# Five of the twelve w_gate slices transposed by DMA in the condition stage instead of by TensorE

## The reference, cut to what matters

```python
out = jnp.einsum('bsd,bdh->bsh', x, W[cat_ids]) + b[cat_ids][:, None, :]   # condition layer
# FFN on xc = act_qdq(out); act_qdq rounds to 16 bits with ONE scale, the maximum over the whole tensor
# lpbq_dequant rounds a weight to 4 bits with a scale for each block of 32
up   = act_qdq(xc @ lpbq_dequant(w_up).T)
gate = act_qdq(xc @ lpbq_dequant(w_gate).T)
sig  = fixed_qdq_u16(sigmoid(gate))
gate = act_qdq(gate * sig)
o    = act_qdq(gate * up)
y    = x + o @ lpbq_dequant(w_down).T
```

## Time and profile before

| what | value |
|---|---|
| median of 3 runs | 962.78 us (962.12 to 963.32) |
| the profiled execution | 961.0 us, span 959.2 us |
| PE busy | 891.4 us (93%) |
| DVE busy | 655.0 us (68%) |
| ACT busy | 422.2 us (44%) |
| DMA | 254.32 MB, mean 265 GB/s |
| condition stage, with its end | 0 to 139 us of the span |
| gate stage | 142.5 to 394 us |

### The profile page before, as it was taken

The page is one execution under the profiler, slowest core; times in us unless marked ns, Lnnn a source line. Parts: engine busy times, 40 slices in busy tenths (PEclk is TensorE's granted clock), DMA queues, the critical chain, the costliest instruction groups (busy, mean ns, idle before and its releaser), DMA issues.

```text
span 959.2 us, 13055 instructions
## 1 busy us (share of the span) xinstructions
PE 891.4 (93%) x4723; PEld 477.6 (50%) x4723; DVE 655.0 (68%) x773; ACT 422.2 (44%) x454; POOL 3.1 (0%) x12
## 2 busy tenths in 40 slices
PE   8999999999999999999999999980079999999998
PEld 7999994444444444444444444430034444444443
DVE  2349869655667455289899889659986788775511
ACT  1112335223223232299898872229865544444000
POOL 0000000000000000000000000000000000000000
PEclk9999999999999999999999999995589999999999
DMA  8999962643574433789999635999977899987221
GB/s 346 383 406 322 326 238 99 174 154 121 173 253 132 135 129 121 220 315 423 412 385 383 247 139 218 408 421 402 418 286 256 298 339 350 343 303 284 87 88 66
DMA packets 81299, 254.32 MB, mean 265 GB/s; under 512 B 32050, under 2 KB 32050, under 8 KB 77170
## 3 DMA queue, kind: packets, MB, share of 16 engines
q1 hardware_dynamic: 46066, 198.72, 55.2%
q10 hardware_dynamic: 35200, 55.20, 16.5%
HBM read 173.94 MB, written 73.66 MB: 258 GB/s over the span
## 4 chain that ended last, share of the span: by engine, by line
PE 82%; DMA 6%; ACT 5%; DVE 4%; issue 2%; SPq 0%; ACTq 0%; POOL 0%; DVEq 0%
PE bank L807 16%; PE bank L809 16%; PE bank L808 16%; PE bank L751 12%; PE bank L842 5%; PE bank L843 5%; PE bank L844 5%; DMA up_extra<-up_scratch 3%; ACT umag L688 2%; DVE ocode L1308 2%; ACT ocode L707 2%; PE bank L737 1%; DMA gate_even<-gate_scratch 1%; DMA wt_down<-wparts 1%; PE bias_bank L843 1%
## 5 line engine op out<-in xcount | busy, mean ns | idle before, releaser
L594 ACT ACTIVATE stage<-bank 128x512 f32<-128x512 f32 x186 | 108.6, 594 | 213.1 <-PE bank L809 164.8
L1069 DVE TENSOR_REDUCE tile_max<-stage 128x1 f32<-128x1536 f32 (+1 forms) x62 | 108.4, 1748 | 34.4 <-ACT stage L594 31.2
L807 PE MATMUL bank<-xq_head,wt_up 128*128 x336 | 127.4, 379 | 0.9 <-ACT stage L594 0.9
L807 PE MATMUL bank<-xq_head,wt_gate 128*128 (+1 forms) x336 | 127.4, 379 | 0.3 <-DVE xq_head L1056 0.3
L808 PE MATMUL bank<-xq_head,wt_up 128*128 x336 | 127.3, 379 | 0.0
L809 PE MATMUL bank<-xq_head,wt_up 128*128 x336 | 127.3, 379 | 0.0
L808 PE MATMUL bank<-xq_head,wt_gate 128*128 (+1 forms) x336 | 127.3, 379 | 0.0
L809 PE MATMUL bank<-xq_head,wt_gate 128*128 (+1 forms) x336 | 127.3, 379 | 0.0
L751 PE MATMUL bank<-xt,w_ring 128*128 128x128 f32 x1024 | 120.8, 277 | 0.2 <-DMA w_ring<-in_L_cond_W_dram 0.2
L751 PEld LDWEIGHTS bank<-xt,w_ring 128*128 128x128 f32 x1024 | 118.4, 194 | 0.5 <-issue 0.5
L842 PE MATMUL bank<-wt_down,o_even 128*128 128x512 f16 x192 | 72.8, 379 | 1.8 <-DVE y_out L1328 1.5
(11 more groups left out here) (189 smaller groups left out, 1311.8 us busy)
## 6 DMA issues: line engine op xcount, KB each, us to landing
up_ring<-up_scratch SPq DMA_DIRECT2D x54, 768.0 KB, 7.0
w_ring<-in_L_cond_W_dram SPq DMA_DIRECT2D x32, 1024.0 KB, 5.8
gate_scratch<-stage ACTq DMA_DIRECT2D x32, 768.0 KB, 3.3
gate_ring<-gate_scratch SPq DMA_DIRECT2D x32, 768.0 KB, 8.7
up_scratch<-stage ACTq DMA_DIRECT2D x30, 768.0 KB, 7.5
product_scratch<-prod_ring SPq DMA_DIRECT2D x19, 768.0 KB, 7.0
back_ring<-product_scratch SPq DMA_DIRECT2D x19, 768.0 KB, 13.0
gate_even<-gate_scratch SPq DMA_DIRECT2D x16, 768.0 KB, 7.7
```

The lines of the kernel that those rows point to most:

```text
L594: nc.scalar.activation(stage[:, q % 2, n % PIECE_TILES, :], up_bank(i, n), ACT.Copy)\
L807: nc.tensor.matmul(bank, w_hi, x_hi, start=(k == 0), stop=False)
L1069: V.tensor_reduce(tile_max[:, side, bass.ds(Q * i + q, 1)], stage[:, q % 2, :, :].rearrange("p t c -> p (t c)"), AX.X, ALU.max, apply_abso ...
```

## The change

Slices 0 to 4 of w_gate (`FLIPPED = 5`) are transposed by DMA, two issues a slice, one for each half, on ACT's queue, straight into `wt_gate`. The ten issues stand in the last eight batches of the condition stage: one behind the high part in each batch of chunk 6 and one in each of the first three of chunk 7, and three behind the last copy of x. PE turns slices 5 to 11, all seven ahead of gate chunk 0, over five banks instead of six (the sixth and seventh take the first two banks again, when ACT has copied them). No turns stand between the tiles any more. Tiles 0 to 4 of gate chunk 0 wait for their slice's two DMAs (`wgate_flipped`, 32), later ones for `w_copied`; tile 3 also waits until all five banks have been copied.

```diff
-TURNED = 7
+FLIPPED = 5
-        TURN_BANKS = (wt_bank, bias_bank, psum[5], psum[4], psum[3], psum[2])
+        TURN_BANKS = (wt_bank, bias_bank, psum[5], psum[4], psum[3])
-            bank = TURN_BANKS[n if n < len(TURN_BANKS) else n % 2]
+            bank = TURN_BANKS[(n - FLIPPED) % len(TURN_BANKS)]
...
+            def flip_half(n, h):
+                act.wait_ge(w_low, n + 1)
+                act.dma_start(wt_gate[:, h, :, n * P:(n + 1) * P], wparts[:, n, h, :], transpose=True)\
+                    .then_inc(wgate_flipped[n], 16)
...
+                    if isinstance(i, int) and i == CHUNKS - 2:
+                        flip_half(r // 2, r % 2)
...
             for r in range(BPC):
                 copy_xt(CHUNKS - 1, r, False)
                 if r == 0:
                     high_part(0, WSLICES - 1, WSLICES - 1, 0)
+                for at in range(BPC + r, BPC + r + 1 if r < BPC - 1 else 2 * FLIPPED):
+                    flip_half(at // 2, at % 2)
-            for n in range(2):
+            for n in range(FLIPPED, FLIPPED + 2):
                 copy_wt(n)
...
-                    if first and n < WSLICES - TURNED:
-                        copy_wt(TURNED + n)
...
-                    if first:
-                        pe.wait_ge(w_copied, max(n + 1, len(TURN_BANKS) if n >= 2 else 0))
+                    if first and n < FLIPPED:
+                        pe.wait_ge(wgate_flipped[n], 32)
+                        if n == 3:
+                            pe.wait_ge(w_copied, len(TURN_BANKS))
+                    elif first:
+                        pe.wait_ge(w_copied, max(n - FLIPPED + 1, len(TURN_BANKS)))
                     tile_matmul(i, i, n, wt_gate, first)
-                    if first and n < WSLICES - TURNED:
-                        turn_w(TURNED + n)
```

More of the change, by code:

```diff
@@ L277, in adaln_ffn @@
         wt_ready = [sem(f"wt_ready{n}") for n in range(SLICES)]
+        wgate_flipped = [sem(f"wgate_flipped{n}") for n in range(FLIPPED)]
         wscale_ready = sem("wscale_ready")
@@ L541, in copy_wt @@
             def copy_wt(n):
-                act.wait_ge(w_turned, n + 1)
+                act.wait_ge(w_turned, n - FLIPPED + 1)
                 nc.scalar.activation(wt_gate[:, :, :, n * P:(n + 1) * P], turn_bank(n), ACT.Copy).then_inc(w_copied, 1)
@@ L567, in _ @@
             cond_chunk(4, False, 1)
-            with act.Fori(5, CHUNKS - 1) as i:
+            with act.Fori(5, CHUNKS - 2) as i:
                 cond_chunk(i, False, 0)
+            cond_chunk(CHUNKS - 2, False, 0)
             for r in range(BPC):
@@ L580, in _ @@
                     .then_inc(xcode_scalar, 1)
-            for n in range(2, TURNED):
+            for n in range(FLIPPED + 2, WSLICES):
                 copy_wt(n)
@@ L757, in turn_w @@
             def turn_w(n):
+                at = n - FLIPPED
                 pe.wait_ge(w_low, n + 1)
-                if n >= len(TURN_BANKS):
-                    pe.wait_ge(w_copied, n - 5 if n < len(TURN_BANKS) + 2 else n - 1)
-                elif TURN_BANKS[n] is psum[3]:
+                if at >= len(TURN_BANKS):
+                    pe.wait_ge(w_copied, at - len(TURN_BANKS) + 1)
+                elif TURN_BANKS[at] is psum[3]:
                     pe.wait_ge(cond_copied, B)
-                elif TURN_BANKS[n] is psum[2]:
-                    pe.wait_ge(cond_copied, B - 1)
-                elif TURN_BANKS[n] is psum[4] or TURN_BANKS[n] is psum[5]:
+                elif TURN_BANKS[at] is psum[4] or TURN_BANKS[at] is psum[5]:
                     pe.wait_ge(x_copied, B)
@@ L816, in gate_chunk @@
                 for n in range(NT):
-                    if first:
-                        pe.wait_ge(w_copied, max(n + 1, len(TURN_BANKS) if n >= 2 else 0))
+                    if first and n < FLIPPED:
[4 more added lines that the diff above has]
+                        pe.wait_ge(w_copied, max(n - FLIPPED + 1, len(TURN_BANKS)))
                     tile_matmul(i, i, n, wt_gate, first)
-                    if first and n < WSLICES - TURNED:
-                        turn_w(TURNED + n)
             pe.wait_ge(ident_made, 2)
-            for n in range(TURNED):
+            for n in range(FLIPPED, WSLICES):
                 turn_w(n)
```

## The result

The changed kernel takes 969.52 us (median of 6 runs, 964.75 to 970.91), the kernel before 963.05 us in the same comparison: 1.0053 of it, with a 95% interval of 1.0041 to 1.0066. (The ratio of the two medians is a little larger, 1.0067; this text goes by 1.0053, which is 5.1 us.) It was forecast at 960.5 us, faster. The profiled execution took 969.79 us, with a span of 968.0 us.

A forecast was written before the change was run, and what follows sets the result against it. PE was taken to set the pace, with DMA transfers close behind. Five turns removed save 2.24 us and all else costs 0, so 962.78 - 2.24 = 960.5 us; range 959.8 to 963.6 us.

The forecast's parts named there:

- What bounds the kernel: Condition and gate stages: PE sets the pace, with DMA engines close behind at 0.87 of their time from 104 to 128 us.
- the five turns: Gate chunk 0, between tiles: five PE turns of w_gate go, pitch 3.04 to 2.59 us, saving 2.24 us.
- Turns ahead of tile 0: Before gate chunk 0: still seven turns; both reused banks are free in time, so price 0.
- ACT after the stage: Behind the codes: five copies of turned slices, done by about 148, before tile 3 at 150.8; price 0.
- later stages: After gate chunk 0: stages start by what PE's tiles release, so the 2.24 us should go through to the end.
- The transfers: Condition stage: each transpose occupies all 16 DMA engines 0.64 to 1.45 us, nearer 1.3; free share and early loads absorb it.
- c = 1.45: Condition stage: c is the us one transpose occupies all 16 DMA engines; at 1.45 five transposes leave 5.5 us of backlog.
- the far bound: DMA transfers: nothing else moves while a transpose is on its way, 2.5 us each, the median landing time.
- Ten issues on ACT's queue: Condition stage: issues hold ACT 1.30 us each, 13 us beside PE; price 0, covered by 0.7 us at the tightest.
- w_up behind them: After the transposes: w_up's load lands at about 146.4 to 147.9, before DVE reads it at 148.15; 5 us more are covered.
- new waits on PE: Gate chunk 0: slices 3 and 4 land by 143.7 and 146.7, before their tiles at 150.8 and 153.4; price 0.
- B: Condition stage, rival: transposes delay x and condition weights; at 2.5 us each, 5.2 us of waits, 965.8 us; chance 13%.

## Why the prediction was wrong

*What bounds the kernel, and the five turns:* right. The pitch is 2.59 us, gate chunk 0 is 2.24 us shorter where nothing comes late (2.0 us in the changed kernel), and the kernels that keep the gain and in which PE waits for no load and no copy come out 0.17 to 0.26% below before, where 0.233% was worked out.

*Turns ahead of tile 0, ACT after the stage, later stages:* nothing of their own. The late copies of turned slices, which hold PE's sixth and seventh turn for 3.2 us, come from ACT's held queue.

*The transfers:* the step that failed, "Up to c = 1.45 PE loses nothing". I priced a transpose by a share of the engines' time, as if its traffic could be laid beside the loads'. In the runs it is the time of the engine that is furthest behind that counts: landings of 12.7 to 23.5 us where 2.5 was the far bound, 34 GB/s for about 6 us, x 13.3 us on its way where 5.7 + 5.5 in hand were allowed. The plain copies, which have the same bytes, fit my sum; the transposes do not. The trace of before had the sign. One of its transposes, issued at 175.32, landed after 4.3 us instead of 2.5, and from 176 to 178 us it has

```profile
q10 hardware_dynamic: 524, 0.12, 97.0%
q8 instruction: 1, 0.02, 4.8%
```

that is, engines busy with 0.12 MB of transposes while one of them fetched code. By the packets, that fetch lasts from 176.55 to 178.10, and 13 transpose packets that start about 177.3 all end at 178.97. I took only the busy time from such stretches, and did not ask why the engines were busy with next to nothing moved.

*Ten issues on ACT's queue:* the second failed step. I took the longest issue of the trace, 1.97 us, as the bound, "Price 0, covered by 0.7 us at the tightest". In these runs an issue was short only while the transposes ahead of it landed. With landings of 15 to 23 us the fifth or later one waits, for 9.41 us in the first profile, and ACT with it.

*PE's clock:* not in the prediction at all, and so put at nothing. The first profile of the changed kernel bears that out; in the second, and in that of the ten added transposes, the clock fell in a wait of 3.5 and of 4.5 us and stayed at the lower level for 6.8 us, which cost about 1.3 and 2.2 us more.

*w_up behind them, new waits on PE:* right in their result; DVE bore a w_up that came 4.4 us late in the kernel with all transposes behind the loads, and no tile waited for a slice.

*Rivals:* B was the nearest, slower by condition loads that come late, at 965.8 us against 969.52. Its price of 2.5 us a transpose was too low, and it lacked ACT. The trace bore it out more than the 13% that I gave it. The estimate worked out there from the Trainium skill's 1309 ns a block ("VectorE: DVE Perf Modes", "The three transpose paths"), 979 us, was too high as a time. The rule of the Trainium skill's same page ("Rules for kernel authors") to use TensorE where a PSUM destination will do is borne out by the changed kernel, 0.5% slower, but not by the two in which SP issues the transposes, 0.2 to 0.3% faster. "Advanced Engine Details and Errata", "X-Bar Transpose (TRN2)", of the Trainium skill speaks of wavefronts of 16 rows in a transpose. The stops seen here, with one engine at work and the rest standing, would fit work that goes in step over the engines, but no run here shows the wavefronts themselves.

*Still open:* why one engine falls behind by several us in some executions. In before at 176 us it was a fetch of code; from 112 to 121 us of the changed kernel the profile shows no such packet. How many transposes ACT's queue takes before it holds was not measured by itself either. Four went through in the first profile and six in the second; in both, and with the ten added ones, three of those issued earlier had not landed when the first long issue began.

## What to carry to other kernels

A DMA transpose beside a stream of large loads is not priced by its bytes: its packets take turns with the loads', and in the longest stop seen here fifteen engines stood while one worked. Put transposes where no load is wanted soon, or behind the loads on the same queue, and rather not on the queue of an engine whose next instruction is on the path; here moving the issues to SP's queue, and so also behind the loads, turned 0.5% slower into 0.2 to 0.3% faster. When a stretch of a trace shows the DMA busy with next to nothing moved, find out why before its busy share goes into a sum.

## What the runs showed of the hardware that was not expected

Beside a write of 128x5120 float16 by GpSimd (4.37 us), five DVE instructions on single columns took 4.58 us, where all five take 0.97 us otherwise. In a wait of PE of 3.5 us in one profile and of 4.5 us in another, the granted clock fell to 0.50 and stayed there for 6.8 us; around one of 2.9 us in a third it stayed at 1.00. Condition weights in rows of 2 KB instead of 8 KB made the kernel before 0.38% slower. And PE's start in the condition stage varies with the first loads: its second batch began between 13.8 and 17.4 us in the profiles, so profiles are compared from a common batch on, not by their spans.
